# A fused cross-attention and mixture-of-experts kernel: the order of GpSimd's scatters, exponential remainders and a bias add within one block

## What is computed

```python
def xattn(x, context, Wq, bq, Wk, bk, Wv, bv, Wo, bo):
    q, k, v = x @ Wq.T + bq, context @ Wk.T + bk, context @ Wv.T + bv   # split into 16 heads
    scores = einsum('bhtd,bhcd->bhtc', q, k) / sqrt(32)
    out = einsum('bhtc,bhcd->bhtd', softmax(scores), v)
    return out @ Wo.T + bo

def ffn(x, W_experts, b_experts, W_router, b_router):
    router_weights = softmax(x @ W_router.T + b_router)      # the 2 largest kept, others 0
    expert_out = einsum('bsd,eod->bseo', x, W_experts) + b_experts
    return einsum('bseo,bse->bso', expert_out, router_weights)

x = x + xattn(layernorm(x), ctx, ...)
x = x + ffn(layernorm(x), ...)
```

## Time and profile before

| what | value |
|---|---|
| median of 3 runs | 1286.14 us |
| lowest and highest run | 1283.73 and 1291.59 us |
| the profiled execution | 1283.73 us, of which the span of its instructions is 1282.0 us |
| its mean granted TensorE clock | 0.979 of full speed |
| PE busy | 1192.9 us, 93% of the span |
| DVE, POOL, ACT busy | 875.2, 747.9, 717.8 us |

### The profile page before, as it was taken

One profiled execution on the slowest core, in us unless ns is written; L12 is line 12 of the kernel. 1 busy time (PEld: TensorE's weight loads), 2 busy tenths in 40 slices (PEclk: granted clock), 3 DMA queues, 4 the chain that ended last, 5 costly groups with the idle time before them and its releaser, 6 DMA issues. The chain is left out here.

```text
span 1282.0 us, 35723 instructions
## 1 busy us (share of the span) xinstructions
PE 1192.9 (93%) x11024; PEld 718.0 (56%) x11025; DVE 875.2 (68%) x1933; ACT 717.8 (56%) x1040; POOL 747.9 (58%) x980
## 2 busy tenths in 40 slices
PE   7887999999999999999999986789899999999997
PEld 4444566566565666656666654444455555555554
DVE  3766789788888888878987875445455555555554
ACT  3337856866876786686697555324333343434343
POOL 5004346766866866776776685756644454455445
PEclk9979999999999999999999998889999999999999
DMA  8843635855765674684566456759998999998886
GB/s 253 266 117 115 181 106 153 239 191 171 211 207 166 199 235 149 188 248 160 178 201 194 155 166 264 283 166 197 200 192 173 176 177 192 189 167 167 169 171 129
DMA packets 135544, 239.19 MB, mean 187 GB/s; under 512 B 18439, under 2 KB 49415, under 8 KB 134279
## 3 DMA queue, kind: packets, MB, share of 16 engines
q1 hardware_dynamic: 102503, 161.24, 42.3%
q0 software_dynamic: 29808, 67.73, 26.0%
q10 hardware_dynamic: 3120, 8.68, 1.9%
HBM read 112.00 MB, written 101.40 MB: 166 GB/s over the span
## 5 line engine op out<-in xcount | busy, mean ns | idle before, releaser
L1896 PE MATMUL S<-we_s,wq_s 128*128 x1620 | 375.7, 382 | 10.8 <-issue 7.5
L1824 POOL DMA_INDIRECT out<-xn,to x135 | 208.9, 1547 | 204.8 <-DMA out<-xn,to 120.2
L1170 POOL TENSOR_TENSOR we_s<-P_s,we_s 128x1024 f16<-128x1024 f32 x96 | 204.6, 2134 | 93.6 <-ACT we_s L936 92.8
L1896 PEld LDWEIGHTS S<-we_s,wq_s 128*128 128x128 f16 x1620 | 158.0, 98 | 178.5 <-issue 19.0
L1835 ACT ACTIVATE wq_s<-PVp 128x512 f16<-128x512 f32 x137 | 81.7, 597 | 263.3 <-PE PVp L1886 245.9
L984 DVE TENSOR_REDUCE mx_sb<-S 128x6 f32<-128x924 f32 x160 | 172.7, 1114 | 22.7 <-PE S L726 19.7
L746 PE MATMUL W<-wo_s,aT_hi 128*128 128x512 f16 x512 | 164.0, 382 | 3.4 <-DVE aT_lo L962 1.7
L708 PE MATMUL W<-we_s,wq_s 128*128 128x512 f16 x512 | 160.3, 385 | 5.5 <-DVE xnT_lo L962 3.6
L1874 DVE SCALAR_TENSOR_TENSOR att<-S,be_s 128x512 f32<-128x512 f32 x135 | 93.4, 692 | 103.8 <-PE S L1896 97.5
L1852 DVE TENSOR_TENSOR wq_s<-PVp,wq_s 128x512 f16<-128x512 f32 x137 | 94.6, 691 | 39.4 <-ACT wq_s L1835 34.8
L818 PE MATMUL PVp<-Vm,we_s 128*128 128x33 f16 x3072 | 118.7, 178 | 0.4 <-issue 0.3
(11 more groups left out here) (208 smaller groups left out, 2046.7 us busy)
## 6 DMA issues: line engine op xcount, KB each, us to landing
P_s<-dispatched SPq DMA_DIRECT2D x139, 260.5 KB
we_s<-we_s SPq DMA_DIRECT2D x186, 128.0 KB
be_s<-in_x SPq DMA_DIRECT2D x16, 1024.0 KB
xR_s<-in_x SPq DMA_DIRECT2D x16, 1024.0 KB, 7.6
out<-xR_s SPq DMA_DIRECT2D x16, 1024.0 KB
wst<-in_weT SPq DMA_DIRECT2D x16, 512.0 KB, 5.9
we_scratch<-wsp SPq DMA_DIRECT2D x16, 512.0 KB
Kst<-k_scratch SPq DMA_DIRECT2D x16, 480.0 KB
```

The source lines that it names most:

```text
L1170: e.tensor_tensor(Pst[1][:, r:r + 2, :], exps(n), Pst[0][:, r:r + 2, :], ALU.subtract).then_inc(pldp, 1)
L1824: e.indirect_dma_start(out, bass.IndirectOffsetOnAxis(ap=to[u][:, :], axis=0), yw[u % YW], None, bounds_check=N - 1, oob_is_err=False, com ...
L1896: m = e.matmul(Yp[:, u % 2, :], gT[u % 2][xp][:, k, :], we_s[:, bass.ds(n * WN + (wp * KC + k) * D, D)], start=(c == 0), stop=(c == 11))
```

## The change

Only the list in `pool_slot` changes, for the slots in which `pool_S1` of `bm1` runs. `pool_PL(bp1, 8)` moves ahead of `pool_S1(bm1, 0)`. `pool_BX(b, 3)` moves ahead of `pool_S1(bm1, 1)`. `pool_S1(bm1, 2)` moves behind `pool_NC(b, 1)` and `pool_RQ(b)`, to where `pool_S1(bm1, 3)` stood, and `pool_S1(bm1, 3)` moves behind `pool_PL(bp2, 0)`, to the end of the slot. `pool_SC` and `pool_SD` keep their places among the others. No instruction, wait or buffer is added or taken away.

```diff
--- before.py
+++ after.py
@@ -1691,27 +1691,26 @@
             pool_S1(e, bm2, 7)
         if on_bp1:
             pool_PL(e, bp1, 7)
+            pool_PL(e, bp1, 8)
         if early1:
             pool_S1(e, bm1, 0)
-        if on_bp1:
-            pool_PL(e, bp1, 8)
+        elif on_bm1 and bm1.here(NB - 3):
+            pool_SC(e, bm1)
+        if on_b:
+            pool_BX(e, b, 3)
         if early1:
             pool_S1(e, bm1, 1)
-        elif on_bm1 and bm1.here(NB - 3):
-            pool_SC(e, bm1)
-        if on_b:
-            pool_BX(e, b, 3)
-        if early1:
-            pool_S1(e, bm1, 2)
         if on_b and not b.last:
             pool_NC(e, b, 1)
             pool_RQ(e, b)
         if early1:
-            pool_S1(e, bm1, 3)
+            pool_S1(e, bm1, 2)
         elif on_bm1 and bm1.here(NB - 3):
             pool_SD(e, bm1)
         if on_bp2:
             pool_PL(e, bp2, 0)
+        if early1:
+            pool_S1(e, bm1, 3)
```

More of the change, by code:

```diff
@@ L1693, in pool_slot @@
             pool_PL(e, bp1, 7)
+            pool_PL(e, bp1, 8)
         if early1:
             pool_S1(e, bm1, 0)
-        if on_bp1:
-            pool_PL(e, bp1, 8)
-        if early1:
-            pool_S1(e, bm1, 1)
         elif on_bm1 and bm1.here(NB - 3):
@@ L1704, in pool_slot @@
         if early1:
-            pool_S1(e, bm1, 2)
+            pool_S1(e, bm1, 1)
         if on_b and not b.last:
```

## The result

The changed kernel takes 1305.88 us (median of four runs, 1305.13 to 1308.86; the profiled execution, 1306.47, is not one of the four) against 1285.39 us before (1283.73 to 1291.59 with a fourth run added). The ratio is 1.0154, 95% interval 1.0117 to 1.0193: slower by 20.5 us, where 1287 was forecast and 1295 was the range's upper end. Run once more later, beside other kernels of the study on one chip, the ratio was 1.0090 (1.0058 to 1.0123). It is slower by about 1 to 1.5%.

The account below looks back on a forecast made before the run. PE, busy 93% of the span, was taken to bound the kernel. All terms were 0 except 1.2 us for the scatters' data: 1286.1 + 1.2 = 1287.3, rounded 1287 us, range 1280 to 1295.

Parts of the forecast that it names:

- The replay of POOL: Slot 9's POOL list replayed in the new order, each step at its own duration; POOL's busy time and other engines' work stay.
- PL 8 back to back: PL 8 directly follows PL 7 on POOL, 1.2 us earlier; its near user comes 12.5 us after its old end; gain nothing.
- the idle time before NC 1: POOL's idle time ahead of NC 1, waiting for ACT's norm, grows from 5.7 to 6.9 us as S1 2 leaves.
- PL 0's wait of 1.20 us: PL 0 on POOL starts at 552.07 after 1.20 us idle as before, released by ACT.
- POOL's loop turn: Turn of POOL's hardware loop, behind S1 3 in every second slot; no row prices it; taken as 0.
- Rival B: Between PL 0 and PL 2, over 1.86 us makes PL 2 late and PE wait; 1% or more slower, at 1300; chance 0.06.
- Rival C: PL 8's earlier end is worth its time if PE or ACT were held by it: 13.8 us faster, 1272.3 us; chance 0.04.
- S1 3 behind PL 0: The scatter ends at 555.36 in the gap before PL 2 at 556.06, leaving 0.70 us; cost taken as 0.
- The data in the burst: S1 3's data meets the load burst from 556 us that PE's MX waits for: 0.1 us a slot, 1.2 us over twelve.
- rival A: The scatter lands inside the load burst: 0.70 us a slot, 8.4 us, 1294.5 us; PE's restack wait 1.7 us; chance 0.08.

Follow-up runs that it names:

- the first profile: The changed kernel against the kernel before, its first profiled execution: 1306.47 us; the median of four other runs is 1305.88 us, ratio 1.0154.
- the second profile: The changed kernel, unaltered, run again on chip C against the kernel before: 1300.38 us against 1290.02, ratio 1.0090.

## Why the prediction was wrong

**The replay of POOL was right, step by step.** PL 8 back to back, the idle time before NC 1 (6.92 us, forecast 6.9), PL 0's wait of 1.20 us, S1 3 0.16 us behind it, POOL's loop turn hidden: all as written. Rival B did not happen: PL 2 is released by ACT. Rival C neither.

**The step that failed is "S1 3 behind PL 0", priced at 0.** It asked what the scatter does to POOL's next step and to the DMA engines, and took for granted that an instruction on POOL acts on nothing else. "Nothing is added or removed, so [...] the other engines' work stay" held for their work, but not for their waits. The missing term is the held signal of PV w = 7: 8.7 - 3.0 = 5.7 us in eight slots at PE's AT step, 0.71 us a slot. Over all twelve slots PE waits 12.4 us there against 4.4 before: 8.0 us, in eleven of the slots, where the term stood at 0. The chain is: PV's increment 0.85 us late, PH 2 on ACT as late, behind it ATh, DVE's remainder of AT, PE's last AT transpose.

**The data in the burst, forecast 1.2 us.** SP's loads also wait for PV's increment, so the burst begins 0.84 us later behind the matmuls (1.13 against 0.29). PE's wait for the restack rose from 8.3 to 10.6 us in the first profile and to 9.3 in the second, 1.33 and 1.16 us a slot, between the 1.04 of the forecast and the 1.7 of rival A. How much of this is the scatter's data and how much the late start wasn't separated. Over the twelve slots PE's wait for the restack is 12.1 us against 10.0, and 10.7 in the second profile: 2.1 and 0.7 us. That 1.2 lies between is luck, as far as the reason is a different one.

**A part that no step had: the clock.** In three of the slots the wait for the restack passed 2 us (2.13, 2.01 and 2.27 us). PE's timeline of the third, and the stretches behind each (us, busy us by engine, the granted clock, DMA share, GB/s):

```profile
492.72 0.95 PE L726 MATMUL S<-Kst,we_s 96*128 96x154 f16 x6 [2.27 <-DMA we_s<-we_s]
```

```profile
301.50:304.90 3.40, 3.40 (x14) 1.69 (x13) 2.40 (x3) 2.00 (x4) 3.27 (x3) 0.50 0.24 88
397.10:400.50 3.40, 3.40 (x13) 1.68 (x12) 2.11 (x2) 1.68 (x3) 3.00 (x3) 0.50 0.22 85
492.70:496.10 3.40, 3.38 (x17) 2.28 (x18) 1.12 (x1) 0.60 (x2) 2.98 (x4) 0.50 0.24 95
525.00:530.00 5.00, 5.00 (x77) 3.48 (x75) 3.40 (x6) 5.00 (x8) 4.59 (x8) 1.00 1.06 335
```

The granted clock is at half, 1.2 GHz, for 3.4 us each time, with PE busy throughout: 1.7 us lost, three times, 5.1 us. Before, the clock stayed at full from 257 to 630 us, where no wait exceeded 1.8 us. In the second profile of the change no such wait reached 2 us (1.9 at most) and the clock stayed at full from 257 to 630 us; there the slots cost less. The length of the wait alone does not decide it: with the small DMA behind PL 0, nine waits of 2.3 to 3.9 us were followed by such a stretch in five cases only, and with S1 3 alone moved one wait of 1.93 us was.

**The sum.** From PL 0 of block 2 to PL 0 of block 14, twelve slots, the kernel before takes 550.5 us (183.62 to 734.14) and the changed one:

```profile
184.47 2.13 POOL L1170 TENSOR_TENSOR we_s<-P_s,we_s 128x1024 f16<-128x1024 f32 x1 [2.89 <-ACT we_s L936]
...
748.99 2.13 POOL L1170 TENSOR_TENSOR we_s<-P_s,we_s 128x1024 f16<-128x1024 f32 x1 [1.32 <-ACT we_s L936]
```

564.5 us, 14.0 more. They are made up of PE's wait at the AT step, 8.0; of its wait for the restack, 2.1; of its busy time, 539.8 against 534.9 us for the same instructions, 4.9, the clock's part; less a wait of 1.0 us (L708, no releaser shown) that only the kernel before has. In the second profile the slots take 558.3 us (183.65 to 741.90), 7.8 more: 8.3 at the AT step and 0.7 for the restack, less the same 1.0, and no part of the clock.

Of the remaining 8.8 us of the first pair of spans, 5.7 lie in phase 2, between its first and its last expert matmul: 432.6 us before and 438.3 after. Other kernels of the study, all with an unchanged phase 2, have 425.8 to 439.2 us there, and these two ends belong to one and the same file, the kernel with the restack first, on chips B and C. I take the 5.7 us for such a difference between executions and chips. That one of this size exists is shown; that it is the one here is argued. The other 3.1 us, ahead of and behind the twelve slots, are not explained. That the ratio fell from 1.0154 to 1.0090 when the change ran again on chip C fits it, and the clock's part, which came in one profile and not in the other, fits as well.

**The range and the chances.** The upper end, 1295, was built from rows on POOL and the DMA engines. The bound of the unknown was missing because the unknown wasn't seen: 0.06 stood for slower by more than 1%, and the mechanism named there was not the one that came.

## What to carry to other kernels

When an indirect DMA on GpSimd is moved, look not only at what it delays on GpSimd but at which TensorE step ends while it executes, and who waits for that step's semaphore: a gap that is free on GpSimd is free for arithmetic, and may not be for a scatter. Put scatters where the TensorE signals that fall due have no waiting reader. Whether a wait for the critical signal, placed ahead of the scatter, would win back the loss was not tried where signals are held; such a wait has its own price, 0.4 us a slot here. Compare variants on one chip: of the three here, one never showed the effect, and three experiments run on it could not test the theory they were made for. A wait that the profile shows on the bounding engine, here the restack's, was worth more than the whole shuffle of GpSimd's list: 1% from one line's place in SP's list, on both chips on which it ran.

## What the runs showed of the hardware

PE's semaphore increment of PV w = 7 was seen 0.8 to 0.9 us after its matmuls' end when POOL's indirect DMA of 0.98 us had begun before that end, and 0.4 us after the scatter's own end; ACT and SP saw it late by about the same amount, and PE's own matmuls went on. POOL arithmetic of the same length and place did nothing of the kind. An indirect DMA of 8 bytes a row did the same as one of 2084 bytes (ACT's wait 0.91 and 0.90 us). It is not general: most increments of MX in the same situation were not late (39 of 41 in the kernel before), and on chip B none of 497 was. Increments due shortly behind a scatter's end can be late as well (PV's at 559.45 in the kernel before, 0.11 us behind the end of S1 4, by 0.44 us). The mechanism behind it is not shown by any run: whether the increment is sent late or the matmuls' completion is, the trace can't tell, since it models the ends of matmuls.
